# A pseudo-inverse iteration written as a linear times a quadratic factor, with its products in all four quarters of the array

## What is computed

```python
def _moore_penrose_pinv(x, num_iters):        # num_iters = 6, x is 64 by 64
    I, V = eye(m), x
    for _ in range(num_iters):
        KV = x @ V
        V = 0.25 * V @ (13.0 * I - KV @ (15.0 * I - KV @ (7.0 * I - KV)))
    return V
...
out = attn1 @ (attn2_inv @ (attn3 @ v))
```

## Time and profile before

| | us |
|---|---|
| median of three runs (lowest, highest) | 1676.68 (1674.38, 1689.81) |
| span of the profiled execution, first to last instruction | 1677.2 |
| mean granted clock of PE, share of full speed | 0.940 |
| busy: PE, DVE, ACT, POOL | 1424.4, 1090.1, 661.6, 300.0 |
| line 749, the products of the iteration: busy on PE | 217.3 |

### The profile page before, as it was taken

The page is one execution under the profiler, slowest core; times in us unless marked ns, Lnnn a source line. Parts: engine busy times, 40 slices in busy tenths (PEclk is TensorE's granted clock), DMA queues, the critical chain, the costliest instruction groups (busy, mean ns, idle before and its releaser), DMA issues.

```text
span 1677.2 us, 45642 instructions
## 1 busy us (share of the span) xinstructions
PE 1424.4 (85%) x19556; PEld 1157.6 (69%) x19588; DVE 1090.1 (65%) x2475; ACT 661.6 (39%) x1365; POOL 300.0 (18%) x334
## 2 busy tenths in 40 slices
PE   5997996779898777898996879988774899999993
PEld 4985773559776555796674549767643799998893
DVE  5776676556756847486667456757855556558872
ACT  3213434232154343213443332144341555557762
POOL 0002130120202202102131020212302021222323
PEclk8799999989999898899998989999997899999997
DMA  7332120010000001000000010000002887888654
GB/s 276 128 133 82 44 78 14 17 37 4 2 3 1 26 2 39 16 4 2 3 13 13 14 41 3 3 3 2 1 1 72 281 297 243 270 268 269 214 173 116
DMA packets 50384, 134.50 MB, mean 80 GB/s; under 512 B 5121, under 2 KB 28929, under 8 KB 49153
## 3 DMA queue, kind: packets, MB, share of 16 engines
q1 hardware_dynamic: 42169, 118.85, 19.9%
q0 software_dynamic: 7152, 9.57, 2.8%
q10 hardware_dynamic: 864, 3.17, 0.5%
HBM read 117.80 MB, written 32.13 MB: 89 GB/s over the span
## 4 chain that ended last, share of the span: by engine, by line
PE 66%; DVE 18%; ACT 8%; issue 3%; DMA 1%; another core or an unknown queue 1%; POOL 0%; SPq 0%; DVEq 0%; ACTq 0%; POOLq 0%
PE bank L2200 13%; PE bank L749 11%; PE bank L2220 6%; PE bank L624 5%; PE bank L633 4%; ACT arena L1708 3%; PE bank L1175 3%; PE bank L609 2%; PE bank L739 2%; PE bank L1589 2%; PE bank L1594 2%; DVE arena L1637 2%; PE bank L1136 2%; DVE arena L1248 1%; ACT arena L1330 1%
## 5 line engine op out<-in xcount | busy, mean ns | idle before, releaser
L749 PE MATMUL bank<-arena 64*64 64x80 f32 (+2 forms) x6400 | 217.3, 226 | 4.5 <-DVE arena L888 2.2
L749 PEld LDWEIGHTS bank<-arena 64*64 64x64 f32 x6400 | 211.2, 137 | 13.5 <-issue 7.9
L1068 POOL TENSOR_TENSOR rstd<-ve,s_neghalf 128x2 f32<-128x2 f32 x48 | 37.5, 780 | 716.0 <-DVE ve L1046 715.2
L2200 PE MATMUL bank<-e_xT,e_w 128*128 128x256 bf16 x1440 | 159.7, 273 | 3.7 <-issue 2.6
L2200 PEld LDWEIGHTS bank<-e_xT,e_w 128*128 128x128 bf16 x1440 | 140.7, 98 | 20.5 <-issue 2.8
L2287 DVE TENSOR_TENSOR e_w<-e_raw,e_w 128x1024 bf16<-128x1024 f32 x90 | 108.9, 1223 | 27.6 <-ACT e_w L2236 27.6
L609 PE MATMUL bank<-c_bf 128*128 128x512 bf16 x230 | 74.2, 473 | 31.2 <-ACT arena L992 10.3
L1012 ACT COPY arena<-bank 128x320 f32<-128x320 f32 (+1 forms) x96 | 37.6, 392 | 157.4 <-PE bank L749 157.0
L2257 ACT ACTIVATE e_silu<-bank 128x256 f32<-128x256 f32 (+1 forms) x192 | 66.1, 344 | 83.9 <-PE bank L2200 76.5
L2307 DVE TENSOR_TENSOR e_h<-bank,e_silu 128x256 f32<-128x256 f32 x120 | 50.6, 422 | 73.5 <-ACT e_silu L2257 69.2
L2236 ACT CAST e_w<-e_raw 128x1024 bf16<-128x1024 f32 x90 | 92.2, 1041 | 0.0
(11 more groups left out here) (317 smaller groups left out, 2977.9 us busy)
## 6 DMA issues: line engine op xcount, KB each, us to landing
e_raw<-E SPq DMA_DIRECT2D x144, 512.0 KB, 8.1
slots<-C_empty SPq DMA_DIRECT2D x13, 1360.0 KB
e_x<-slots SPq DMA_DIRECT2D x15, 272.0 KB, 3.3
w_rest<-W_rest SPq DMA_DIRECT2D x1, 3592.0 KB, 16.8
xz<-xT SPq DMA_DIRECT2D x8, 256.0 KB, 2.8
x<-x SPq DMA_DIRECT2D x8, 256.0 KB, 2.9
ctx<-ctxT SPq DMA_DIRECT2D x8, 256.0 KB, 2.7
tokens<-y SPq DMA_DIRECT2D x8, 256.0 KB, 2.2
```

What stands on the lines that cost most here:

```text
L749: last = pe.matmul(b[r, p * width:(p + 1) * width], lhs[r, 4 * g + p, :], rhs[r, 4 * g + p, :], start=True, stop=True)
L2200: last = pe.matmul(bank[b][:, col:col + wide], w, x, start=j == 0, stop=j == len(terms) - 1)
```

## The change

- A step's cubic in `K` is split as a linear factor times a quadratic one: with `ROOT` the real root of x^3 - 7x^2 + 15x - 13, the step needs `K - ROOT I` (`jt`), `K - LINEAR I` (`jb`), and `st`, which is -0.25 times (`n_qt` plus `CONSTANT` I). There is no running update any more: `jt` and `jz` are written afresh. The number of products and their shapes stay.
- `products` now issues both groups in one call, pair by pair, and with `across` = 1 the second group's halves are crossed: rows 0-63 write partitions 64-127 of bank 1, rows 64-127 write partitions 0-63. The four quarters hold four different heads. `n_kt` and `n_kz` keep `across` = 0. In a step `n_qw` comes before `n_qt`; all waits are for both groups.
- DVE has three operations per step and group instead of four (`jb`, `st`, `jt`); ACT copies `n_rw` as well as `n_qw`.
- `ORDERS` is written anew. From the second dilated step on, the PE list has the same steps in nearly the same order; inside the iteration A's and B's steps alternate differently. `FILLED_WAITS` has base-36 digits, 623 fillers in all in place of 262.

```diff
-    "jt": (F32, PAIRS, M), "wt": (F32, PAIRS, M), "g": (F32, PAIRS, ROWS32),
+    "jt": (F32, PAIRS, M), "jb": (F32, PAIRS, M), "g": (F32, PAIRS, ROWS32),
-CS = [3.25 ** i for i in range(PINV_ITERS + 1)]
+ROOT = float(next(r.real for r in np.roots([1.0, -7.0, 15.0, -13.0]) if abs(r.imag) < 1e-9))
+LINEAR, CONSTANT = 7.0 - ROOT, 13.0 / ROOT
...
-            for _ in range(int(FILLED_WAITS.get(name, NOT_FILLED)[bat])):
+            for _ in range(int(FILLED_WAITS.get(name, NOT_FILLED)[bat], 36)):
...
-            def products(name, g, lhs, rhs, width):
-                b = bk.claim(pe, f"{name}_{g}")
+            def products(name, lhs, rhs, width, across):
+                banks = [bk.claim(pe, f"{name}_{g}") for g in range(2)]
                 for p in range(4):
-                    for r in HALVES:
-                        last = pe.matmul(b[r, p * width:(p + 1) * width], lhs[r, 4 * g + p, :], rhs[r, 4 * g + p, :],
-                                         start=True, stop=True)
-                last.then_inc(bk.filled(f"{name}_{g}"), 1)
+                    for g, b in enumerate(banks):
+                        for u, r in enumerate(HALVES):
+                            to = HALVES[u ^ (g & across)]
+                            last = pe.matmul(b[to, p * width:(p + 1) * width], lhs[r, 4 * g + p, :], rhs[r, 4 * g + p, :],
+                                             start=True, stop=True)
+                        if p == 3:
+                            last.then_inc(bk.filled(f"{name}_{g}"), 1)
...
+                    if g == 0:
+                        pe.wait_ge(sem(f"n_shift{s}"), due("n_shift", bat, 2 * i + 2))
+                        for h in range(2):
+                            bk.await_emptied(pe, f"{z}_{h}")
+                        products(f"n_qw{i}", n["jt"], n["jz"][:, :, cols], cols.stop - cols.start, 1)
                     yield
-                    products(f"n_qw{i}", g, n["jt"], n["jz"][:, :, cols], cols.stop - cols.start)
+                    if g == 0:
+                        for h in range(2):
+                            bk.await_emptied(pe, f"{t}_{h}")
+                        products(f"n_qt{i}", n["jz"][:, :, 0:M], n["jb"], M, 1)
...
+                    dve.tensor_tensor(n["jb"][:, q], part(b, M), shifted(1), ALU.add).then_inc(bk.emptied(name), 1)
...
-                    dve.tensor_tensor(n["st"][:, q], part(b, M), n["wt"][:, q], ALU.add)\
+                    dve.scalar_tensor_tensor(n["st"][:, q], part(b, M), -0.25, shifted(2), ALU.mult, ALU.add)\
                         .then_inc(bk.emptied(f"n_qt{i}_{g}"), 1)
...
-                for g in range(2):
+                for name, to in ((f"n_qw{i}", n["qw"]), (f"n_rw{i}", n["jz"])):
```

More of the change, by code:

```diff
@@ L71 @@
 FILLED_WAITS = {
[L72 to L84, removed]
+    "n_max1_0": "03303030",
+    "n_max3_0": "81878787",
+    "n_negT": "j3303030",
+    "n_xT": "0f0f0f0f",
+    "d_s1_0": "60404040",
+    "d_s2_0": "60606060",
+    "d_coef0": "0b0b0b0b",
+    "g_m00_0": "0k0k0k0k",
+    "g_negT": "b0b0b0b0",
+    "g_s01_0": "73737373",
+    "g_o0": "7f7f757f",
+    "g_s11_0": "50505050",
+    "g_o1": "07070707",
+    "m_xT": "g2g2g2gk",
 }
@@ L187 @@
[L187 to L191, removed]
@@ L217 @@
[L217 to L221, removed]
+    "pe": """0x4 1x2 0x1 1x2 0x2 1x1 0x4 1x1 0x3 1x1 0x5 1x3 0x8 1x1 0x1 1x8 0x6 1x6 0x5 1x14 0x1 1x1 0x11 1x5 0x1 1x1 0x6 1x5 0x6
@@ L757, in pe_nystrom @@
                 bk.await_emptied(pe, f"n_aT_{g}")
-                products("n_kt", g, n["az"][:, :, 0:M], n["aT"], M)
+                if g:
+                    products("n_kt", n["az"][:, :, 0:M], n["aT"], M, 0)
                 yield
-                products("n_kz", g, n["aT"], n["az"], M + DH0)
+                if g:
+                    products("n_kz", n["aT"], n["az"], M + DH0, 0)
             t, z = "n_kt", "n_kz"
@@ L775, in pe_nystrom @@
                     yield
-                    bk.await_emptied(pe, f"n_qt{i}_{g}")
-                    bk.await_emptied(pe, f"n_qw{i}_{g}")
+                    if g == 0:
+                        for h in range(2):
+                            bk.await_emptied(pe, f"n_qt{i}_{h}")
+                            bk.await_emptied(pe, f"n_qw{i}_{h}")
                     if not end:
                         yield
-                        products(f"n_rt{i}", g, n["qw"][:, :, 0:M], n["st"], M)
+                        if g == 0:
+                            products(f"n_rt{i}", n["qw"][:, :, 0:M], n["st"], M, 1)
                     yield
-                    products(f"n_rw{i}", g, n["st"], n["qw"][:, :, cols], cols.stop - cols.start)
+                    if g == 0:
+                        products(f"n_rw{i}", n["st"], n["qw"][:, :, cols], cols.stop - cols.start, 1)
                 t, z = f"n_rt{i}", f"n_rw{i}"
@@ L899, in dve_nystrom @@
                 b = bk.await_filled(dve, f"n_kt_{g}")
-                dve.tensor_copy(n["jt"][:, q], part(b, M)).then_inc(bk.emptied(f"n_kt_{g}"), 1)
+                dve.tensor_tensor(n["jt"][:, q], part(b, M), shifted(0), ALU.add).then_inc(sem(f"n_shift{s}"), 1)
             for i in range(PINV_ITERS):
-                end = i == PINV_ITERS - 1
-                back = -CS[i] ** 3 / 13.0
                 yield
@@ L921, in dve_nystrom @@
                     q = slice(4 * g, 4 * g + 4)
-                    cols = slice(M, M + DH0) if end else slice(0, M + DH0)
-                    if not end:
+                    if i < PINV_ITERS - 1:
                         yield
                         b = bk.await_filled(dve, f"n_rt{i}_{g}")
-                        dve.scalar_tensor_tensor(n["jt"][:, q], part(b, M), back, n["jt"][:, q], ALU.mult, ALU.add)\
-                            .then_inc(bk.emptied(f"n_rt{i}_{g}"), 1)
+                        dve.tensor_tensor(n["jt"][:, q], part(b, M), shifted(0), ALU.add).then_inc(sem(f"n_shift{s}"), 1)
                     yield
-                    b = bk.await_filled(dve, f"n_rw{i}_{g}")
-                    dve.scalar_tensor_tensor(n["jz"][:, q, cols], part(b, cols.stop - cols.start), back,
-                                             n["jz"][:, q, cols], ALU.mult, ALU.add)\
-                        .then_inc(bk.emptied(f"n_rw{i}_{g}"), 1)
             yield
```

104 lines of the change are left out of this document (56 added, 48 removed).

## The result

The changed kernel takes 1741.19 us (median of 4, 1737.13 to 1748.19) against 1679.4 us for the kernel before: ratio 1.0367, 95% interval 1.0325 to 1.0409. It is slower, and the prediction (1645 us, 1605 to 1690) has the wrong sign. A run's time lies 1.8 to 1.9 us above its span (1748.19 against 1746.3 in the profiled execution), so the forecast's base, the span of 1677 us, was short by about that much; it does not bear on the rest.

A forecast was written before the change was run, and what follows sets the result against it. PE's products were taken to bound the iteration's stretch. From the 1677 us span, 24 us (four rounds of 5.9 us) and 8 us for fillers came off: 1645 us, range 1605 to 1690.

The forecast's parts named there:

- The pair: On PE, a weight load and matmul falls from 32.2 to 16.1 ns, since four pairs run side by side instead of two.
- The rival that the quarters take turns: Pairs on the same rows take turns, a step takes 6.2 us instead of 4.1: 1717 us; chance 0.08.
- A batch alone gains nothing: Steps one batch runs alone: products, lag, two DVE operations and PE's start sum to 2.06 us per half step, as now.
- Here PE is full, at half the old price: A's last two and a half steps mixed with B's first one and a half: PE full, 10.6 us.
- ACT's copies: Two copies of 0.39 us beside a half step's second product, costed at nothing; 0.8 us per step if uncovered.
- The clock in the half-empty steps: Rival: the clock falls, PE's part doubles, 1 us on each of 14 half steps a round: 1701 us; chance 0.04.
- A's projections are over by then: 4.5 us more: A's dilated projections, now between B's last product and `n_o` and before `n_out`, are over earlier, saving 4.5 us.
- The stretch by hand: Round two from A's first `n_kt` to B's last `n_rw`, followed through the new lists: 66.3 us against 67.66.
- The fillers: 361 more at 0.236 us ahead of waits, 85 us of PE, mostly hidden and holding the clock up: -8 us.

## Why the prediction was wrong, point by point

Round two's stretch in the changed kernel again, cut otherwise: up to B's `n_qw0`, from there to A's `n_o` (A's and B's half steps alternate here), from A's `n_o` on (B alone); then the products' group in the middle part.

```profile
393.25:432.84 39.59, 33.69 (x794) 29.87 (x795) 18.27 (x47) 11.95 (x29) 0.00 (x0) 0.72 0.01 3
432.84:447.43 14.59, 9.90 (x485) 8.90 (x488) 8.29 (x24) 5.24 (x17) 0.00 (x0) 1.00 0.02 4
447.43:471.42 23.99, 19.45 (x549) 15.46 (x548) 16.23 (x38) 8.22 (x21) 3.13 (x4) 1.00 0.02 3
...
L756 PE MATMUL bank<-arena 64*64 64x64 f32 (+2 forms) x480 | 9.9, 225 | 4.7 <-ACT arena L1024 2.0 <-issue 1.9 <-DVE arena L935 0.8
```

- **The pair** (32.2 to 16.1 ns): right. 64 pairs and their tail take 1.25 us, 1.03 + 0.22 as predicted. The rival that the quarters take turns fell; the Trainium skill, TensorE: Matmul & The Clock Gate, section The mechanism, which spoke for it, does not hold for these quarters. Line 756 is busy for 161.8 us and not 125, since part of it runs at 1.2 GHz and each half step ends in a tail (at the full clock 480 pairs are busy for 9.90 us, 20.6 ns each, in the rows above).
- **"A batch alone gains nothing"**: right in kind. Only the last term was short: PE starts 0.20 us after DVE, not 0.05. 1.25 + 0.67 to 0.76 + 0.02 + 0.20 makes 2.1 to 2.2 us instead of 2.06, up to 2 us a round over the 14 half steps that a batch runs alone. DVE, as forecast, ends the largest part of the idle time ahead of line 756 (22.8 of 53.3 us).
- **"Here PE is full, at half the old price"** (A's and B's mixed steps, 10.6 us): failed, and at the full clock (second and fourth row above). PE idles for a third of the mixed part: 14.59 us, or 30.4 ns a pair, hardly less than the 32.2 of two quarters. ACT's copies, which I had costed at nothing on the path, end most of the idle time that has a named cause (2.0 us). I had also read the 16.96 us of the earlier trace rows as A and B covering each other; the old list runs them there one after the other, each covered by its own stagger.
- **The clock in the half-empty steps** (chance 0.04, 56 us): failed. I had it on one window of 4 us with PE busy in 2.57; a single window in which the clock stayed up was no evidence for a run of such steps. The stretch fell to 0.86. What it cost is known only roughly, see the stretch below.
- **"A's projections are over by then: 4.5 us more"**: failed. From B's last `n_rw` to B's transposes it was 17.9 us (471.42 to 489.30) instead of the 12.7 that the forecast needs (17.2 in the kernel before). The projections, drawn forward, start POOL's products just when DVE copies `g`. With the copies on ACT it was 12.8 us, about the forecast's figure, and the whole kernel 15.5 us faster: the step was right but for the copies and for the clock there, 0.71 with them on DVE and 1.00 with them on ACT. I had costed the copies as unchanged and looked at POOL's busy time (3.14 us) only inside the stretch.
- **The stretch by hand** (66.3 us): 78.2. The three windows above say where the 11.9 us missing lie: 39.59 us instead of 31.8 up to B's `n_qw0`, 14.59 instead of 10.6 in the mixed part (and one of A's half steps, which I had counted there, runs in the first), 23.99 instead of 23.9 from A's `n_o` on, where B is alone. In the first part the fillers in front of B's `n_max3` are 1.7. That leaves 6.1 us for the clock, which is at its low level in 22 of these 39.59 us, and for all else that I had too short there; the 8.5 us that the rounds of one kernel would price the clock at are more than this.
- **The fillers** (-8 us): wrong sign on the kernel before (+18), near zero in the changed one (+6 when they go). The new list also takes the nine fillers from in front of `n_aT`: A's `n_y` then runs at 1.2 GHz (6.98 against 3.70 us), and with the fillers back, at 3.71 to 4.44 us, they cost about what it gains. Idle time ahead of a wait is not free room: the bank or the moment may come late.
- **The order of work**: not a term of mine at all. I followed the new lists only through the stretch and held the rest as "the same list". The new order with the old arithmetic costs 81 to 84 us, though in lists that were not made for it, and in the changed kernel the rests grew by 21.

So the steps that failed are the full PE in the mixed part, the clock, the copies beside POOL and the order outside the stretch. Not settled: how the 81 to 84 us split over the moves in the lists, how much of the rests' growth is order and how much clock, and whether alternating half steps in an otherwise old list would gain.

## What to carry to other kernels

Halving an engine's work inside a chain that has only just been covered by it turns the work into waits; look for what was hidden behind the old length first, and count the clock as one of the things that hung on it. When a step is moved, ask what its end releases on other queues (here POOL's products), and who shares something with those. Before counting on one batch to cover another, read from the engine's list whose half step follows whose. Rounds of the same list at different clocks inside one profile are a free, if rough, measurement of what the clock costs.

## What the runs showed of the hardware

- A DVE copy between two tiles in SBUF waits for a running POOL product: 1.87 and 1.89 us instead of 0.22, in B of rounds two to four; in round one B's first copy starts 0.17 us ahead of POOL's product and takes 0.21, the second 1.97. A's copies, beside an idle POOL, take 0.22 in every round. The group's mean hides it, and the wait is booked as busy time of the copy. ACT's copies took 0.30 each, beside the same products or not. The Trainium skill, SBUF — State Buffer, section Who interferes with whom, says that a DVE copy, where it runs in a mode with two ports, and a GpSimd instruction lock one shared pair of ports, each for its whole length, and that ACT never waits; the trace agrees in who waits and for how long, while no run shows the mode.
- The clock went down after stretches in which PE was busy in 60% (4.06 of 6.80 us) and 79% (8.08 of 10.20), both at 1.00; in the kernel before it was at 1.00 in a window with 64% and stayed there in the 4 us behind it. The busy share alone did not foretell it.
